# Seven products in place of eight in a Performer's first MLP product, with its sums on GpSimd and VectorE and the condition's split moved forward

## What is computed

```python
def _L0_mix_ref(x, Wqkv, bqkv, Pmat, Wproj, bproj, W1, b1, W2, b2, g1, be1, g2, be2):
    ...
    x = x + attn @ Wproj + bproj          # 1250x512
    h2 = layernorm(x, g2, be2)
    mlp = jax.nn.gelu(h2 @ W1 + b1, approximate=False) @ W2 + b2   # W1 512x1024, W2 1024x512
    return x + mlp
```

## Time and profile before

| what | value |
|---|---|
| three runs | 2309.66, 2314.97, 2318.09 us (median 2314.97) |
| profiled execution, its own time | 2313.01 us |
| its span | 2311.2 us |
| TensorE busy | 2286.3 us, 99% |
| VectorE, ScalarE, GpSimd busy | 62%, 42%, 55% |
| first product, first to last group | 330.7 to 398.7 us of the span |

### The profile page before, as it was taken

The page is one execution under the profiler, slowest core; times in us unless marked ns, Lnnn a source line. Parts: engine busy times, 40 slices in busy tenths (PEclk is TensorE's granted clock), DMA queues, the critical chain, the costliest instruction groups (busy, mean ns, idle before and its releaser), DMA issues. The chain is left out here.

```text
span 2311.2 us, 29926 instructions
## 1 busy us (share of the span) xinstructions
PE 2286.3 (99%) x10169; PEld 1514.1 (66%) x10169; DVE 1426.7 (62%) x2532; ACT 975.5 (42%) x1694; POOL 1276.5 (55%) x1731
## 2 busy tenths in 40 slices
PE   8999999999999999999999999999999999999998
PEld 4566645457677777777877777877767776544443
DVE  7778660615876763777673677675477665634445
ACT  4437732222765331666331476432276533212221
POOL 2005403142666981566894366796266687637775
PEclk9999999999999999999999999999999999999999
DMA  6400221320666210466210266410066611679517
GB/s 175 149 19 25 80 63 46 111 77 14 159 173 180 93 60 1 114 166 158 86 44 24 51 174 163 136 45 24 1 157 163 164 76 36 234 235 350 191 47 241
DMA packets 136882, 260.39 MB, mean 113 GB/s; under 512 B 53564, under 2 KB 55980, under 8 KB 134390
## 3 DMA queue, kind: packets, MB, share of 16 engines
q1 hardware_dynamic: 88520, 152.11, 22.4%
q0 software_dynamic: 46864, 104.03, 16.2%
q10 hardware_dynamic: 1346, 2.33, 0.4%
HBM read 213.17 MB, written 32.20 MB: 106 GB/s over the span
## 5 line engine op out<-in xcount | busy, mean ns | idle before, releaser
L118 POOL DMA_DIRECT2D cols<-w x720 | 353.3, 499 | 220.1 <-PE psum L1074 173.8
L1074 PE MATMUL psum<-cols,rows 125*128 125x256 f32 x1600 | 368.3, 379 | 0.0
L1061 PE MATMUL psum<-g_k_cols,g_q_cols 128*125 128x512 f32 (+1 forms) x960 | 360.8, 513 | 0.2
L1074 PEld LDWEIGHTS psum<-cols,rows 125*128 125x128 f32 x1600 | 303.1, 190 | 36.2
L1156 DVE CUSTOM_DVE_ANT_0 g_prob<-psum,ln_count 125x1250 f32<-125x1250 f32 x160 | 233.7, 1461 | 102.5 <-PE psum L1061 102.2
L1061 PEld LDWEIGHTS psum<-g_k_cols,g_q_cols 128*125 128x125 f32 x960 | 179.4, 187 | 165.2 <-issue 155.5
L1254 ACT ACTIVATE g_prob<-g_prob,g_row_max 125x1250 f32<-125x1250 f32 x160 | 215.8, 1348 | 124.5 <-DVE g_row_max L1156 122.5
L1170 DVE STREAM_TRANSPOSE w<-g_prob 128x1280 f32<-128x1280 f32 x160 | 241.5, 1509 | 34.7 <-DMA cols<-w 26.3
L1260 ACT ACTIVATE g_prob<-g_prob,g_row_max 125x1250 f32<-125x1250 f32 x160 | 215.6, 1347 | 67.8 <-DVE g_row_max L1145 67.5
L580 POOL TENSOR_TENSOR rows<-rows,g_bias_rows 125x512 f32<-125x512 f32 x40 | 50.0, 1270 | 186.1 <-DVE rows L570 186.1
L3456 PE MATMUL psum<-m_ew,m_x_cols 128*64 128x256 f32 (+1 forms) x576 | 150.1, 492 | 0.0
(11 more groups left out here) (460 smaller groups left out, 4568.1 us busy)
## 6 DMA issues: line engine op xcount, KB each, us to landing
cols<-w POOLq DMA_DIRECT2D x720, 80.0 KB, 3.2
cols<-w SPq DMA_DIRECT2D x560, 80.0 KB, 3.5
w<-in_L_gnn_m_w SPq DMA_DIRECT2D x8, 1024.0 KB
slot_rows<-p_kf SPq DMA_DIRECT2D x1, 7344.0 KB, 32.8
rows<-slot_rows SPq DMA_DIRECT2D x54, 136.0 KB, 7.2
m_ew<-in_L_ffn_expert_w SPq DMA_DIRECT2D x4, 1536.0 KB, 9.6
xbuf<-xn_scratch SPq DMA_DIRECT2D x20, 250.0 KB
slot_outputs<-slot_rows SPq DMA_DIRECT2D x1, 5000.0 KB
```

What stands on the lines that cost most here:

```text
L118: return eng.dma_start(out, in_, allow_slow_non_contiguous=True)
L1061: ins = pe.matmul(psum[0:P, at:at + width], q_cols[:, h, t * P:(t + 1) * P], k_cols[:, h, start:start + width], start=True, stop=True)
L1074: ins = pe.matmul(c.bank(6 + g % 2, 256).rearrange("p (u a i) -> p u a i", u=2, a=SIDE), rows[0:P, j, h * 128:(h + 1) * 128], turned_keys[ ...
```

## The change

The first product is cut in four runs: half of the columns (0 to 749, or 750 to 1249) by half of the outputs. In a run both operands are two by two blocks, and seven block products replace eight: 14 pairs (p, u) of two products over k, each 375 or 250 columns wide. The sums that this wants:

- of the weights: eight GpSimd instructions over 128x512, after the last `out_mm`, ahead of everything else that GpSimd has left;
- of the columns: per half three VectorE instructions over 128x750 (128x500) and two over 128x375 (128x250);
- of the results: per run ten VectorE additions from PSUM, two ScalarE copies from PSUM, two Gelus from PSUM and six Gelus in place.

The split of `cond` moves to VectorE's projection loop, one instruction behind each norm of the tiles 2 to 6. The split of `cond_w` moves to GpSimd, behind the weight sums. SP loads `z` and the inputs after the runs in place of before, and the bias row earlier.

```diff
-    H_BANKS = [2, 3, 4, 5, 0, 1, 6, 7]
+    H_BANKS = {1: (2, 3), 2: (2, 3), 5: (4, 5), 3: (4, 5), 6: (0, 1), 7: (6, 7), 4: (6, 7)}
+    H_RUNS = [(half, part) for half in range(2) for part in range(2)]
...
+        def split_cond_w_pool():
+            g = c.pool
+            g.wait_ge(cond_w_in, 128)
+            g.wait_ge(h_weight_sums, 8)
+            for n in range(3):
+                if n:
+                    g.wait_ge(cond_w_ready, 4 + 2 * n)
+                g.tensor_copy(w_split[n], cond_w).then_inc(cond_w_ready, 1)
+                if n < 2:
+                    g.wait_ge(cond_w_ready, 5 + 2 * n)
+                    g.tensor_tensor(cond_w, cond_w, w_split[n], ALU.subtract).then_inc(cond_w_ready, 1)
...
             sp.wait_ge(o_mm, NT)
             load(sp, w[2][:], w2_view[:, 0:KC, :]).then_inc(w_in[2], 16)
-            sp.wait_ge(h_turned, 2 * NT)
-            for t in range(INPUT_RING):
-                input_sp(t)
...
             stack_sp()
-            sp.wait_ge(h_mm, GROUPS)
+            sp.wait_ge(h_mm, h_done(2, 3, 1))
             load(sp, w[1][:], w2_view[:, KC:2 * KC, :]).then_inc(w_in[1], 16)
-            sp.wait_ge(h_mm, 2 * GROUPS)
+            sp.wait_ge(h_mm, h_done(3, 4, 1))
+            for t in range(INPUT_RING):
+                input_sp(t)
+            sp.wait_ge(h_mm, h_done(3, 3, 1))
+            for t in range(Z_RING):
+                z_sp(t)
...
+            for r, (half, part) in enumerate(H_RUNS):
...
+                for p in SEVEN_AT:
+                    for u in range(2):
+                        if p == 1:
+                            if r == 0:
+                                pe.wait_ge(h_cols, KC * (NT + 3))
+                            else:
+                                pe.wait_ge(h_act_made, 4 * r - 1 + u)
...
+                        elif p == 2:
+                            pe.wait_ge(h_act_made, 4 * r + 1 + u)
...
+                        if u == 0 and p in (5, 7, 6, 3):
+                            pe.wait_ge(h_weight_sums, 4 * part + {5: 1, 7: 2, 6: 3, 3: 4}[p])
+                        if u == 0 and p in (5, 6, 7, 4):
+                            pe.wait_ge(h_col_sums, 5 * half + {5: 1, 6: 2, 7: 3, 4: 5}[p])
...
+                        if r == 0 and u == 1 and p in (1, 2):
+                            h_turn_pe(1, NT - 3 + p)
...
             for t in range(2, NT):
...
                 if t == 2:
                     divide(Q_STEPS - 1)
+                if 3 <= t < 8:
+                    split_cond_dve(t - 3)
+            h_first_sum_dve(0)
             h_norm_dve(NT - 1)
-            for i in range(10):
-                split_dve(i)
+            v.wait_ge(h_turned, 2 * NT - 2)
+            h_middle_sum_dve(0, 2)
+            v.wait_ge(h_turned, 2 * NT - 1)
+            h_middle_sum_dve(0, 3)
+            v.wait_ge(h_turned, 2 * NT)
+            h_last_sum_dve(0)
+            for r in range(len(H_RUNS)):
+                h_run_dve(r)
...
+                if r == 1:
                     s.wait_ge(parts_in, 192)
+                for u in range(2):
+                    s.wait_ge(h_mm, h_done(r, 1, u))
+                    s.copy(out[:, 2 + u, n0], c.bank(H_BANKS[1][u], width)).then_inc(h_act_made, 1)
...
+            g.wait_ge(out_mm, Q_STEPS)
+            for part in range(2):
+                wt = w[1 - part]
+                g.wait_ge(w_in[1 - part], 32)
...
+                g.tensor_tensor(s1, a21, a22, ALU.add).then_inc(h_weight_sums, 1)
+                g.tensor_tensor(s3, a11, a21, ALU.subtract).then_inc(h_weight_sums, 1)
+                g.wait_ge(h_weight_sums, 4 * part + 1)
+                g.tensor_tensor(s2, s1, a11, ALU.subtract).then_inc(h_weight_sums, 1)
+                g.wait_ge(h_weight_sums, 4 * part + 3)
+                g.tensor_tensor(s4, a12, s2, ALU.subtract).then_inc(h_weight_sums, 1)
+            split_cond_w_pool()
```

More of the change, by code:

```diff
@@ L1583, in performer, with h_weight_sum, h_col_sum @@
         cond_w_parts_flat = cond_w_parts[:].rearrange("p n d -> p (n d)")
-        def split_dve(i):
+        rows_flat = rows[:].rearrange("p t d -> p (t d)")
+        kf_flat = kf_mem[:].rearrange("p a f -> p (a f)")
+        h_cols_of = (q_cols, k_cols)
+        def h_weight_sum(part, i):
+            at = part * 4 * D + (i - 1) * D
+            return shared[:, at:at + D].rearrange("p (c o) -> p c o", c=2)
+        def h_col_sum(half, i):
+            width = HALVES[half][1]
+            mem, at = {1: (edge_sum_mem, 0), 2: (kf_flat, 0), 3: (kf_flat, 2 * HALVES[0][1])}[i]
+            return mem[:, at:at + 2 * width].rearrange("p (c n) -> p c n", c=2)
@@ L1587, in split_dve, with h_last_sum, h_parts, h_done @@
+        def h_last_sum(half, k):
+            mem, at = ((kf_flat, 4 * HALVES[0][1]), (rows_flat, KC * N))[k]
+            return mem[:, at:at + HALVES[half][1]]
+        def h_parts(half):
+            start, width = HALVES[half]
+            return slice(start, start + width), slice(start + width, start + 2 * width)
+        def h_done(r, p, u):
+            return 14 * r + SEVEN_AT[p] + u + 1
+        def split_cond_dve(i):
             v = c.dve
-            which, i = divmod(i, 5)
-            rest, parts = ((cond[:, :], c_split), (cond_w, w_split))[which]
@@ L1620, in stack_sp @@
                 for n in range(3):
-                    sp.wait_ge(part_made, 3 * which + n + 1)
+                    if which == 0:
+                        sp.wait_ge(part_made, n + 1)
+                    else:
+                        sp.wait_ge(cond_w_ready, 5 + 2 * n)
                     for i, pair in enumerate(PART_PAIRS):
@@ new lines, in h_last_sum_dve, with h_run_dve @@
+        def h_last_sum_dve(half):
+            v = c.dve
+            n0, n1 = h_parts(half)
+            v.wait_ge(h_col_sums, 5 * half + 2)
+            for k in range(2):
+                v.tensor_tensor(h_last_sum(half, k), cols[:, 2 + k, n0], h_col_sum(half, 2)[:, k], ALU.subtract).then_inc(
+                    h_col_sums, 1)
+        def h_run_dve(r):
+            v = c.dve
+            half, part = H_RUNS[r]
+            out = h_cols_of[part]
+            width = HALVES[half][1]
+            n0, n1 = h_parts(half)
+            for u in range(2):
+                v.wait_ge(h_mm, h_done(r, 6, u))
+                v.wait_ge(h_act_made, 4 * r + 1 + u)
+                v.tensor_tensor(out[:, u, n1], out[:, 2 + u, n0], c.bank(H_BANKS[6][u], width), ALU.add).then_inc(h_dve_made, 1)
+            if r == 1:
+                h_first_sum_dve(1)
+            for u in range(2):
+                v.wait_ge(h_mm, h_done(r, 7, u))
+                v.wait_ge(h_dve_made, 10 * r + 1 + u)
+                v.tensor_tensor(out[:, 2 + u, n1], out[:, u, n1], c.bank(H_BANKS[7][u], width), ALU.add).then_inc(h_dve_made, 1)
+                v.wait_ge(h_dve_made, 10 * r + 3 + 2 * u)
+                v.tensor_tensor(out[:, 2 + u, n1], out[:, 2 + u, n1], c.bank(H_BANKS[5][u], width), ALU.add).then_inc(
+                    h_dve_made, 1)
+            if r == 1:
+                h_middle_sum_dve(1, 2)
+                h_middle_sum_dve(1, 3)
+            for u in range(2):
+                v.wait_ge(h_mm, h_done(r, 4, u))
+                v.tensor_tensor(out[:, 2 + u, n0], out[:, u, n1], c.bank(H_BANKS[4][u], width), ALU.add).then_inc(h_dve_made, 1)
+            if r == 1:
+                h_last_sum_dve(1)
+            for u in range(2):
+                v.wait_ge(h_mm, h_done(r, 3, u))
+                v.tensor_tensor(out[:, u, n1], out[:, u, n1], c.bank(H_BANKS[3][u], width), ALU.add).then_inc(h_dve_made, 1)
```

156 lines of the change are left out of this document (100 added, 56 removed).

## The result

The changed kernel took 2319.84 us (median of 20 runs, 2313.36 to 2325.55), the kernel before 2313.92 in 20 runs beside them: a ratio of 1.0023, with a 95% interval of 1.0014 to 1.0032, or +5.3 us (3.2 to 7.4). That is no change by the bound of 0.5%, as forecast, and inside the range.

A forecast was written before the change was run, and what follows sets the result against it. TensorE, busy 99% of the span, was taken as the bound. From the profiled 2313.01 us, -8.2 + 9.9 + 0.8 + 0.1 = +2.6 gave 2315.6, stated as 2316 us; range 2305 to 2324.

The forecast's parts named there:

- first product, with the waits in it: First product in four runs: 8.2 us saved, less waits of 0.8 for ScalarE's copy and 0.1 between later runs.
- waits ahead of the turns: Projection stage: TensorE waits 9.9 us for VectorE's late norms, in four turns, of tiles 3 to 6.
- What bounds it: Whole kernel: TensorE is busy 99% of the span, so a change gains only what it takes off TensorE's path.
- What is saved: First product: seven block products for eight take 58.9 us in place of 67.1, saving 8.2 us.
- the copy's wait: First run of the first product: TensorE waits 0.8 us at p = 2 for ScalarE's copy of p = 1.
- The 0.1 at the run borders: Borders between later runs of the first product: TensorE waits 0.1 us, from the same scheme in the graph network.
- GpSimd's instructions: GpSimd's sums and splits: 1.27 us a sum, 3.9 a subtraction, 2.1 a cast over 2048 columns.
- The hold: Projection stage: VectorE stands until GpSimd's current instruction ends, then does its whole work; 12.7 us of holds in all.
- the two rivals in which fewer are held: Projection stage: the split holds nothing (2306 us, chance 0.17), or only casts leave VectorE free (2310.2 us, chance 0.13).
- the slower one: Turns 3 to 6: GpSimd's cast and subtraction take 5.1 us each, +14.0 us, 2327 us; chance 0.10.
- Additions that read PSUM: VectorE additions reading PSUM beside one SBUF tensor were taken as not held by GpSimd; no size given.
- the rest: Holds shared out otherwise (a norm just missing its turn waits 3.9 us more), or an unseen wait in the runs; chance 0.10.

The follow-up runs named there:

- the filled wait: The changed kernel with eight unused products of 512 columns put ahead of the turn that waits 7.3 us; 2316.68 us, ratio 1.0012 to the kernel before.
- the repeat: The changed kernel run again as it is, for a second profile, beside the kernel before on that chip; 2323.10 us against 2317.74, ratio 1.0021.

## Why the prediction was right, and where it was not

| term | forecast | measured in the stretch |
|---|---|---|
| first product, with the waits in it | -8.2 + 0.8 + 0.1 = -7.3 | -7.30 |
| waits ahead of the turns | +9.9, in four turns | +7.96, in two |
| clock behind the long wait | none | +2.35 (1.5 in the second profile); 1.34 net of a wait that it covered |
| sum | +2.6 | +3.0 |

**What bounds it.** Right: in every run the stretch moved by what TensorE waited, was spared, or ran at the lower clock, and by nothing else. The last of the three was not in the prediction.

**What is saved.** Right, to 0.2 us. The stretch gives -7.30 as -8.0 for the products (67.2 us before; 60.72 less 0.86 for two turns and 0.68 for the wait now) and +0.68, where -8.2, +0.8 and +0.1 were forecast; that the sums agree to the hundredth is chance. In the first product a pair stands 1.26 and 0.84 us behind the last, as in the graph network, and the copy's wait was 0.51 (0.68 with its fixed share) in place of 0.8, in the one place named. The 0.1 at the run borders showed no wait.

**GpSimd's instructions.** The cast was taken at 2.1 and took 1.88; the subtraction at 3.9 and took 4.05 to 4.12; a sum at 1.27 and took 1.26 to 1.72 where VectorE held it. The Trainium skill, GPSIMD Engine Reference, section Performance versus the Vector engine, has 4.5 us for a two-input addition of 2048 columns; this case's subtraction lies between that and the 3.9 worked out from the row of 16 partitions, nearer to the latter.

**The hold.** Right in kind and in size: end of GpSimd's current instruction, then all but 0.1 to 0.3 us of VectorE's own time, for casts as for subtractions and on 18 partitions. The holds of VectorE come to 11.9 us (0.2, 0.2, 1.05 and 3.8 at the norms; 1.1, 3.9 and 1.7 at the splits), against 12.7 forecast. So the two rivals in which fewer are held fall by the rows of 317.12 and 328.52, and the slower one by a cast of 1.88. Additions that read PSUM are not held (0.67), as was assumed there without a row.

**The step that was mis-sized** is "TensorE waits 9.9 us, in four turns, of tiles 3 to 6 (about 1.6, 3.9, 3.2, 1.2)". Measured were 0.28, 7.32, 0 and 0. The hold was laid out in one direction only. VectorE's subtraction held GpSimd's second cast (3.00 in place of 1.88), by which the second subtraction began at 324.26, 0.01 ahead of the norm of tile 4. That norm met the whole of it, and the split behind it met a cast where a subtraction of 3.9 had been laid out. Two waits came together in one turn, GpSimd was done sooner in VectorE's order, and the last holds (1.3 of a split, 0.2 of a norm) never happened. The prediction had named this among the rest, at 0.10: "a norm that just misses its turn waits 3.9 more". At full clock the waits come to 8.96 (the stretch of 100.70 with the filled wait, less 99.04, plus 7.30), so the term was too high by 0.9, about as much as the holds were (12.7 against 11.9).

**The step that was missing**: a wait was priced at its length. Behind the wait of 7.3 us TensorE ran at the lower clock, which cost 2.35 us; 1.0 of them covered the next wait, and 1.34 is what the filled wait gave back. The two errors, -0.9 and +1.3, have opposite signs, and that the sums nearly agree is partly luck.

**What stays open.** The time moved by 5.3 us (3.2 to 7.4), and by 4.9 (2.1 to 7.4) in the repeat, the stretch by 3.0 and 2.1: at or just below the lower ends. Of the 5.00 us by which the second product starts later in the profile (403.73 against 398.73), 2.00 stood there already when the stretch began (301.69 against 299.69). Behind it TensorE's rows keep their distance for nearly 200 us (+5.42 at 596.40). What the profiled spans differ by besides lies in parts that were not touched, and differs from profile to profile. Some 2 to 3 us are not placed. The granted clocks of all executions say something on them: in the repeat their mean is 0.9971, against 0.9986 before on the same chip, so by estimate up to 3.6 us of the 4.9 is clock (0.00154 of 2318), and only 1.5 of that lies in the profiled stretch. Where the rest of it falls is not shown.

## What to carry to other kernels

Work on GpSimd is not free because GpSimd is idle: lay its instructions beside those of VectorE, and let each hold the other up. Where VectorE has less idle time than one GpSimd instruction lasts (here 1.39 us a tile against 4), move the work to a stretch where VectorE waits anyhow, or cut it into short instructions. Here the same split cost 10.3 us behind the spreads and nothing among them, and in pieces of 512 columns 1.9. And TensorE, made to wait for several microseconds, can lose more than the wait; read the granted clock behind it.

## What the runs showed of the hardware that was not expected

- The hold is mutual and goes by whole instructions: GpSimd's cast waited 1.1 us for VectorE (3.00 against 1.88), and GpSimd's ten additions of the bias row took 14.25 us beside the column sums, against 12.26 alone:

```profile
346.84 14.25 POOL L3055 TENSOR_TENSOR xbuf<-xbuf,p_bias_rows 125x512 f32<-125x512 f32 x10 [14.71 <-DVE p_kf L2073]
```

  The Trainium skill, GPSIMD Engine Reference, section Key points, has VectorE's instructions with two SBUF inputs, among others, contend with GpSimd; the trace agrees, and gives the price.
- A GpSimd cast from fp32 to bf16 over 18x2048 takes 1.88 us, less than half of the subtraction's 4.05.
- After 7.3 us of idle time TensorE's next product ran 1.9 us long in one profile and 1.0 in another; behind the waits of 1.75 us and less in the projection stage no slow product was seen. The length of one wait is not all that counts: in the kernel before, TensorE waited only 1.45 and 0.78 us shortly ahead of and in a stretch with a granted clock of 0.79, late in the program:

```profile
2047.00:2055.00 8.00, 7.22 (x37) 3.27 (x38) 0.00 (x0) 1.17 (x2) 0.15 (x1) 0.79 0.93 332
```

  The Trainium skill, TensorE: Matmul & The Clock Gate, section Part 1: The HAM clock gate, says that TensorE's clock is gated by how busy it has lately been, and that the count of slow products differs from run to run of one kernel; the trace agrees in both (0.92 against 1.00 with the time filled, 5.32 against 4.45 us from one projection's start to the turn). The prediction had not asked this of its own waits.
